# A second attention with stationary values, normalised before the turn, and four small changes

## The reference, cut to what matters

```
q, k, v = x @ wq[e].T, x @ wk[e].T, x @ wv[e].T
attn    = softmax(where(mask, q @ k.T / 4, -1e30))
outs[e] = (attn @ v) @ wo[e].T
fused   = concatenate(outs)
result  = silu(fused @ w_gate.T) * (fused @ w_up.T)
```

## Time and profile before

| | us |
|---|---|
| median of 3 runs | 416.32 |
| lowest, highest | 416.05, 422.2 |
| the profiled execution | 418.84 |
| its span, first to last instruction | 417.0 |
| TensorE busy | 398.4 (96%) |
| VectorE busy | 239.5 (57%) |
| ScalarE busy | 171.4 (41%) |
| GpSimd busy | 50.8 (12%) |

### The profile page before, as it was taken

The page is one execution under the profiler, slowest core; times in us unless marked ns, Lnnn a source line. Parts: engine busy times, 40 slices in busy tenths (PEclk is TensorE's granted clock), DMA queues, the critical chain, the costliest instruction groups (busy, mean ns, idle before and its releaser), DMA issues.

```text
span 417.0 us, 7793 instructions
## 1 busy us (share of the span) xinstructions
PE 398.4 (96%) x3100; PEld 332.8 (80%) x3100; DVE 239.5 (57%) x734; ACT 171.4 (41%) x290; POOL 50.8 (12%) x107
## 2 busy tenths in 40 slices
PE   8999999998899999999999989999999999999993
PEld 8978888787568767686747778998998999869783
DVE  1567656613368676777456387576558304687353
ACT  1246441742466546453513663354233320551420
POOL 7134010340000000100001310000000200304002
PEclk9999999999999999999999999999999989999998
DMA  7999600000299000000000997044221000000001
GB/s 200 260 194 223 142 11 1 2 0 4 61 242 283 12 2 0 2 0 2 2 0 11 272 265 221 17 128 132 67 67 57 2 0 2 3 2 2 2 0 38
DMA packets 28658, 30.53 MB, mean 73 GB/s; under 512 B 4868, under 2 KB 24074, under 8 KB 28623
## 3 DMA queue, kind: packets, MB, share of 16 engines
q1 hardware_dynamic: 28072, 29.82, 29.1%
q10 hardware_dynamic: 390, 0.22, 0.2%
q0 software_dynamic: 160, 0.01, 0.0%
HBM read 29.63 MB, written 0.39 MB: 72 GB/s over the span
## 4 chain that ended last, share of the span: by engine, by line
PE 83%; DVE 7%; ACT 3%; DMA 2%; issue 2%; POOL 1%; SPq 0%; DVEq 0%; POOLq 0%
PE ps L1474 75%; PE ps L1478 7%; DMA front<-in_x 2%; PE ps L1486 2%; DVE bn L984 1%; DVE wide L1349 1%; POOL rstd L509 1%; DVE mv L987 1%; ACT front L670 1%; DVE xn L999 1%; DVE front L1136 0%; DVE front L1135 0%; ACT front L686 0%; ACT front L766 0%; DVE front L1129 0%
## 5 line engine op out<-in xcount | busy, mean ns | idle before, releaser
L1474 PE MATMUL ps<-halves 128*128 128x512 f32 (+1 forms) x360 | 80.5, 378 | 1.3 <-ACT front L716 1.3
L1474 PE MATMUL ps<-front 64*64 64x64 f32 (+3 forms) x912 | 71.7, 265 | 5.1 <-ACT front L772 1.4
L1474 PEld LDWEIGHTS ps<-front 64*64 64x64 f32 (+2 forms) x912 | 64.9, 166 | 13.8 <-issue 4.4
L1474 PE MATMUL ps<-wide,front 128*128 128x192 f32 x432 | 73.7, 332 | 0.0
L1474 PEld LDWEIGHTS ps<-halves 128*128 128x128 f32 x360 | 63.0, 188 | 13.1 <-ACT front L716 1.7
L1474 PEld LDWEIGHTS ps<-wide,front 128*128 128x128 f32 x432 | 72.0, 194 | 1.0 <-issue 0.5
L716 ACT ACTIVATE front<-ps,colc 128x512 f32<-128x512 f32 x60 | 39.6, 688 | 53.0 <-PE ps L1474 52.9
L1478 PE MATMUL ps<-ident,front 128*128 128x128 f32 (+1 forms) x192 | 28.6, 276 | 0.7 <-DVE front L1149 0.4
L1296 DVE SCALAR_TENSOR_TENSOR xn<-ps,small,xn 128x192 f32<-128x192 f32 x28 | 9.8, 410 | 29.7 <-PE ps L1474 29.7
L1478 PEld LDWEIGHTS ps<-ident,front 128*128 128x128 f32 (+1 forms) x192 | 21.2, 138 | 6.3 <-issue 3.0
L1474 PE MATMUL ps<-xT,turned 128*64 128x256 f32 (+1 forms) x96 | 24.0, 474 | 1.5 <-ACT turned L656 1.5
(11 more groups left out here) (268 smaller groups left out, 537.9 us busy)
## 6 DMA issues: line engine op xcount, KB each, us to landing
wide<-in_w SPq DMA_DIRECT2D x8, 576.0 KB, 4.6
wide<-in_w SPq DMA_DIRECT2D x8, 384.0 KB, 6.0
wide<-in_w SPq DMA_DIRECT2D x16, 192.0 KB, 6.3
front<-in_a2w SPq DMA_DIRECT2D x5, 576.0 KB
front<-in_a1w SPq DMA_DIRECT2D x5, 384.0 KB
front<-in_x SPq DMA_DIRECT2D x3, 512.0 KB, 7.8
front<-in_w_qkv SPq DMA_DIRECT2D x2, 576.0 KB, 7.5
front<-in_a1w SPq DMA_DIRECT2D x5, 192.0 KB
```

Of the source, the lines that this page charges most:

```text
L1474: return pe.matmul(o, l, r, start=start, stop=stop)
```

## The change

Second attention. The values are stationary now, in 64x32 tiles (64 keys of one image, a pair's 32 features of which 16 are zeroed for the other head), and the turned probabilities of one head and one image move, 64 columns. So the output is written already turned. It has no column of sums: VectorE normalises the exponentials before they are turned. Scores run two steps ahead, `p1` has three buffers, `oT1` has two, and the first projections of expert 1 stand before the loop.

```diff
-        vbd = take(2, NT, PAIRS, 2, 2 * DH + 1)
+        vz = take(2, NT, PAIRS, 2, 2 * DH)
-        p1 = take(2, PAIRS, 2, S)
+        p1 = take(3, PAIRS, 2, S)
-        oT1 = take(2, T)
+        oT1 = take(2, 2, T)
...
 @@ scalar
+            def oT_out(n):
+
+                e, t = divmod(n, NT)
+                act.wait_ge(s["pv1_mm"], n + 1)
+                if e >= 2 and t == 0:
+                    act.wait_ge(s["wo1_mm"], 2 * (e - 1))
+                act.activation(oT1[0:96, e % 2, :, t * P:(t + 1) * P].rearrange("p c (m i) -> p c m i", m=2),
+                               ps[0:96, 6:8, 0:P].rearrange("p m (c i) -> p c m i", c=2),
+                               ACT.Copy).then_inc(s["oT1_done"], 1)
...
+            qk_out(1, 1)
+            qk_out(1, 0)
+            exp1(1)
             N1 = NT * EA
             for n in range(N1):
                 pT1_out(n)
                 if e < EA - 1:
-                    if t == 0:
-                        qk_out(e + 1, 1 if e == 0 else 0)
-                    elif t == 2:
+                    if t == 0 and e >= 1:
+                        qk_out(e + 1, 0)
+                    elif t == 1:
                         qk_out(e + 1, 2)
                     elif t == 3:
                         v_out(e + 1, 0)
-                if t == 1 and e >= 1:
-                    fT_out(e - 1)
-                if n + 1 < N1:
-                    exp1(n + 1)
+                if n + 2 < N1:
+                    exp1(n + 2)
...
+                if e >= 1 and t == (2 if e < EA - 1 else 0):
+                    fT_out(e - 1)
+                oT_out(n)
 @@ vector
+            def softmax1_out(n):
+
+                x = n % 2
+                pk = p1[:, n % 3].rearrange("p a m j -> p (a m) j")
+                dve.wait_ge(s["exp1"], n + 1)
+                link(dve.tensor_reduce(mx1[:, x, :], pk, AX.X, ALU.add))
+                link(dve.reciprocal(mx1[:, x, :], mx1[:, x, :]))
+                dve.tensor_tensor(pk, pk, mx1[:, x, :].unsqueeze(2).to_broadcast([P, 2 * PAIRS, S]),
+                                  ALU.mult).then_inc(s["p1_done"], 1)
...
             softmax1_in(0)
+            softmax1_in(1)
+            softmax1_out(0)
             N1 = EA * NT
-            for n in range(N1):
-                e, t = divmod(n, NT)
-                if n + 1 < N1:
-                    softmax1_in(n + 1)
-                if n % 2 == 0 and n >= 2:
-                    oT_out(n // 2 - 1)
-                if t == 1 and e >= 1:
-                    fT_low(e - 1)
-                out1(n)
-            oT_out(2 * EA - 1)
+            for n in range(N1 - 1):
+                if n + 2 < N1:
+                    softmax1_in(n + 2)
+                softmax1_out(n + 1)
 @@ tensor
-                if x == 0 and e == 0:
+                if x == 1 and e == 0:
                     pe.wait_ge(s["wt_act"], EA)
-                if x == 1 and e == 0:
                     pe.wait_ge(s["wt_dve"], EA)
...
             def turn1(n):
-                pe.wait_ge(s["exp1"], n + 1)
+                pe.wait_ge(s["p1_done"], n + 1)
...
             def values1(n):
                 e, t = divmod(n, NT)
                 pe.wait_ge(s["pT1_done"], n + 1)
-                pe.wait_ge(s["v1_done"], 2 * e + 1 + t // 2)
+                pe.wait_ge(s["v1_done"], 2 if n == 0 else 2 * e + 1 + t // 2)
                 if n >= 1:
-                    pe.wait_ge(s["o1_done"], n)
-                w = 2 * (2 * DH + 1)
-                for p in range(PAIRS):
-                    ins = mm(ps[:, 7, p * w:(p + 1) * w], pT1[:, n % 2, p, :],
-                             vbd[:, e % 2, t, p].rearrange("p m d -> p (m d)"), True, True)
+                    pe.wait_ge(s["oT1_done"], n)
+                for c in range(2):
+                    for h in range(2):
+                        for g in range(3):
+                            p = 3 * c + g
+                            for m in range(2):
+                                r = slice(DB * m, DB * m + DB)
+                                ins = mm(ps[32 * g:32 * g + 32, 6 + m, S * c:S * (c + 1)],
+                                         vz[r, e % 2, t, p, h, :], pT1[r, n % 2, p, S * h:S * (h + 1)], h == 0, h == 1)
                 ins.then_inc(s["pv1_mm"], 1)
...
             values_in(0, 1)
+            scores1(1)
+            project1(1, 1)
+            project1(1, 0)
             for n in range(N1):
-                if n + 1 < N1:
-                    scores1(n + 1)
-                if n == 0:
-                    project1(1, 1)
+                if n + 2 < N1:
+                    scores1(n + 2)
                 turn1(n)
                 if e < EA - 1:
-                    if t == 0:
+                    if t == 0 and e >= 1:
                         project1(e + 1, 0)
-                        if e >= 1:
-                            project1(e + 1, 1)
-                    elif t == 2:
+                        project1(e + 1, 1)
+                    elif t == 1:
                         project1(e + 1, 2)
+                    elif t == 2 and e >= 1:
+                        join(e - 1, 0)
+                        join(e - 1, 1)
                     elif t == 3:
                         values_in(e + 1, 0)
                         values_in(e + 1, 1)
-                if n >= 1:
-                    turn_o(n - 1)
-                if t == 1 and e >= 1:
+                elif t == 0:
                     join(e - 1, 0)
                     join(e - 1, 1)
-                if e == EA - 1 and t >= 2:
-                    gate_up(t, first)
+                elif t < 3:
+                    gate_up(t + 1, first)
+                else:
+                    pe.wait_ge(s["s1_read"], N1)
+                    gate_up(0, first)
                 values1(n)
-            pe.wait_ge(s["s1_read"], N1)
-            gate_up(0, first)
-            turn_o(N1 - 1)
             gate_up(1, first)
             join(EA - 1, 0)
             join(EA - 1, 1)
```

```diff
+            def values_wide(i):
+
+                pe.wait_ge(s["wv_lo"], 1)
+                pe.wait_ge(s["v0_done"], 3 + i)
+                at, o = slice(i * P, (i + 1) * P), ps[:, 2, 0:3 * P]
+                mm(o, xs0.high[:, at], wvx.high, True, False)
+                mm(o, xs0.high[:, at], wvx.low, False, False)
+                mm(o, xs0.both[:, at], wvx.both, False, False)
+                mm(o, xs0.low[:, at], wvx.high, False, False)
+                mm(o, xs0.lowB[:, at], wvx.both, False, True).then_inc(s["v0_mm"], 1)
...
             for hp in range(PAIRS - 1):
+                if hp in (2, 3):
+                    values_wide(2 * hp - 4)
                 project0(hp + 1)
-                values_in0(hp + 1)
+                if hp + 1 < 3:
+                    values_in0(hp + 1)
+                elif hp in (2, 3):
+                    values_wide(2 * hp - 3)
```

```diff
+            for i in range(NT):
+                for k in range(2):
+                    ins = mm(two_t(6, i), xT[:, k, i * P:(i + 1) * P], wos[:, k, :], k == 0, k == 1)
...
-            keep_busy(25, 2)
+            keep_busy(10, 2)
...
-                    ins = dve.scalar_tensor_tensor(tok[:, i, :], tok[:, i, :], rstd[:, i:i + 1], xn[:, i, :],
+                    ins = dve.scalar_tensor_tensor(tok[:, i, :], two_t(6, i), rstd[:, i:i + 1], xn[:, i, :],
...
+            for c in range(2):
+                link(dve.bn_stats(bn[:, c, :], wvo3[:, 1, c, :]))
+                link(dve.bn_aggr(mv[:, c, :], bn[:, c, :]))
+                ins = dve.scalar_tensor_tensor(wos[:, c, :], wvo3[:, 1, c, :], mv[:, c, 0:1], bc["ln_w"][:, :],
+                                               ALU.subtract, ALU.mult)
```

```diff
-            finish(0)
+            added(0, 2)
+            moments(of(tok), 0)
+            centre(of(tok), of(xn), 0, done="fin_ready")
             dve.wait_ge(s["cls_mm"], 1)
...
-            finish(1)
+            added(2, 1)
+            moments_one(2)
+            added(3, 1)
+            moments_one(3)
+            centre_one(2)
+            centre_one(3)
```

More of the change, by code:

```diff
@@ L137, in vit_tower @@
         mx0 = take(2, B)
+        v0w = take(NT, 3 * P)
         take = carve(front[:, 9600:])
@@ L589, in _ @@
             rsqrt(0, 96, 1)
-            rsqrt(1)
+            rsqrt(1, n=1)
+            rsqrt(1, n=1, first=3)
         @block.scalar
@@ L900, in _ @@
             send(act, 6)
-            send(act, 7)
         @block.vector
@@ L2145, in _ @@
             pe.wait_ge(s["m0_in"], 64)
-            down(hT[:, 0], m0w2, 4, halves=True, tiles=range(2))
+            down(hT[:, 0], m0w2, 4, tiles=range(2), each=True)
             pe.wait_ge(s["selm_done"], 1)
@@ L2155, in _ @@
             ins.then_inc(s["cls_mm"], 1)
-            down(hT[:, 0], m0w2, 4, halves=True, tiles=range(2, NT))
+            down(hT[:, 0], m0w2, 4, tiles=range(2, NT), each=True)
 _INS = {
```

254 lines of the change are left out of this document (122 added, 132 removed).

## The result

The changed kernel takes 412.5 us (median of four runs, 409.79 to 413.96), the kernel before beside it 416.75: a ratio of 0.9865, 95% interval 0.983 to 0.990, so about 1.3% faster, which is less than the 2% that the prediction took for the least that can be told from no change; the interval does exclude no change. Two later groups of runs gave 0.983 (0.979 to 0.987) and 0.9866 (0.983 to 0.991). The profiled execution took 411.31 (span 409.6) against 418.84 (417.0); predicted was 413.2 for it and 411 for the median. One part of the luck is in the executions that were profiled: the pair differs by 7.5 us, the medians of the same group by 4.25, and the ratio stands for 5.6.

What follows compares the result with a forecast made beforehand. TensorE, busy 96% of the span, was taken to bound the kernel. Gains of 3.6 + 1.3 + 0.6 + 0.1 = 5.6 us took the profiled 418.84 to 413.2, the median to 411; range 407.5 to 416, held at 0.8.

Steps and rivals of the forecast that it cites:

- Start of the second attention: Second attention: first projection no longer waits for weight copies, scores at 108.75 instead of 112.02; first turn 117.75, head start spent.
- part 2's 1.3: First attention: wide fp32r value products replace narrow ones, gain 1.3 us, so everything later starts that much sooner.
- The later signs: Second attention: first turns of experts 1 and 3 expected at about 138.0 and 185.1.
- The values: Second attention, each step: 48 records in 64x32 tiles at 22.7 ns, 1.10 us; bounds 1.04 and 1.90.
- rival B: Second attention: small tiles cost 39.5 ns per record, 8 us more in ten steps, 419 in all; chance 0.05.
- VectorE's step: Second attention: VectorE takes 5.26 us per step, 5.4 with two handoffs, from the end of scores to the next turn.
- Step by step: Second attention: expert 0 takes 21.55 us, experts 1 and 2 together end at 186.4, last join at 213.6; gain 3.6.
- a clock of 0.50 inside expert 0: Second attention, expert 0: listed among the signs that would make the forecast wrong, without a size.
- rival A: Second attention: clock falls at 102.8 (1.5), handoffs cost more (1.4), tiles cost 1.29 (1.9); 4.8 back, 415.6; chance 0.25.
- First attention: Wide value records at 160 ns: steps 2 and 3 gain 0.35 each, step 4 1.2; ScalarE delay 0.64; net 1.3.
- Norm of the retention: Layer norm of the last attention: joining 1.05 us earlier, less about 0.45 for making the centred weight; gain 0.6 us.
- Finish: End of the kernel, finishing per tile: last DMA issue at 415.3 against 415.4, gain 0.1 us.

Runs made afterwards that it cites:

- the kernel before with the wait moved: Kernel before, with only the first projection of the second attention no longer waiting for the last weight copies: 415.28 us, 0.9916 of the kernel before.
- undisturbed profile: Profile of the changed kernel run again unaltered, in which the clock did not fall in expert 0: 411.09 us, 0.983 of the kernel before.
- wait: Changed kernel whose first projection of the second attention waits again for the last weight copies: 413.89 us, 0.9907 of the kernel before.
- values: Changed kernel with the first attention's values of pairs 3 to 5 made pair by pair in fp32 as before: 412.8 us, 0.9887 of the kernel before.
- norm: Changed kernel with the retention's scaled products back on VectorE, 25 filler products and no centred weight: 411.42 us, 0.9844 of the kernel before.
- row order: Changed kernel with each step's 48 small records reordered so that neighbours share their half of the rows: 409.38 us, 0.981 of the kernel before.
- early projection: Changed kernel with expert 1's third projection and its ScalarE copies one step sooner, no filler: 411.54 us, 0.979 of the kernel before.
- half multiplication: Changed kernel with VectorE normalising only 32 of every 64 probabilities, part of the computation left out: 406.82 us, 0.971 of the kernel before.
- the two kernels with filler: Changed kernel with unused products in expert 0's waits (409.91 us, 0.9775), and with every hole filled plus the third projection sooner (409.22 us, 0.978).
- the four variants of the second group: Changed kernel with weight wait restored (0.9907), narrow first-attention values (0.9887), retention's norm back on VectorE (0.9844), or small records reordered (0.981).
- The kernel with filler but one larger hole left: Changed kernel with filler ahead of turns and expert 1's third projection one step sooner, no filler ahead of the third turn: 411.63 us, 0.982.

## Why the prediction was right, and where it was right by luck

**Start of the second attention: right.** The first scores end at 107.62 (108.75 less part 2's 1.3 was said), the first turn starts at 116.64 (116.4). VectorE's two inputs and one output ahead of the first turn spend the head start: 16.66 us from the first projection to the first turn in each of the three profiles of the changed kernel, 13.12 in the kernel before with the wait moved. The later signs were met less well: the first turns of experts 1 and 3 were due at 138.0 and 185.1 and came at 139.17 and 183.99 in the first profile, one late by the clock, one early by the cheaper steps.

**The values: the term of the sum that was mis-sized.** 1.10 us per step were taken, 0.74 was measured, below the lower bound of 1.04, which came from 64x64 tiles; rival B (39.5 ns) is out. By the distance of starts it is less still, 0.67 (198.65 to 199.32 in the first profile). The Trainium skill, TensorEngine Tiling (Array Packing), Key Properties, says that switching the mode drains the engine, and I had put an estimate of 0.1 us per step beside it. The trace agrees: where a piece in full 128x128 tiles stands ahead of the new products, its distance to the next piece grew by 0.10, from 3.43 to 3.53 for the two projections (138.61 to 142.14) and from 2.60 to 2.70 for the values' projection. Behind the third projection (1.87 for 1.88) and the join (3.67 both times) nothing was added; these ran in 128x64 and 96x128 tiles. That draining is what the 0.10 is made of no run shows.

**VectorE's step: 5.4 taken, 5.10 measured.** Its timeline in the undisturbed profile never waits:

```profile
116.93 0.75 DVE L1164 TENSOR_TENSOR front<-ps,causal 128x256 f32<-128x256 f32 x2
117.60 0.41 DVE L1166 TENSOR_TENSOR front<-ps,causal 128x256 f32<-128x256 f32 x1
118.05 0.95 DVE L1170 TENSOR_REDUCE front<-front 128x12 f32<-128x768 f32 x1
119.03 0.96 DVE L1171 TENSOR_TENSOR front<-front 128x768 f32<-128x768 f32 x1
119.91 0.95 DVE L1179 TENSOR_REDUCE front<-front 128x12 f32<-128x768 f32 x1
120.89 0.23 DVE L1180 RECIPROCAL front<-front 128x12 f32<-128x12 f32 x1
121.15 0.96 DVE L1181 TENSOR_TENSOR front<-front 128x768 f32<-128x768 f32 x1
122.03 0.75 DVE L1164 TENSOR_TENSOR front<-ps,causal 128x256 f32<-128x256 f32 x2
```

122.03 - 116.93 = 5.10. The subtraction and the multiplication have 0.96 as their length, but what follows starts 0.88 after them; and the two handoffs (0.14) are hidden by the second step of depth. Lengths overlap: a sum over a queue that never waits has to be made from starts.

**Step by step, undisturbed.** From first turn to first turn expert 0 took 20.83 for 21.55 predicted; experts 1 and 2 22.40 each for 23.55 (steps of 5.78, 5.35, 5.92, 5.35 for 6.2, 5.4, 6.55, 5.4: the values in two of them, and joining, with 3.67 + 1.54 instead of 3.70 + 2.04); expert 3 to its join about 22.1 for 23.5. The second step of an expert, 5.35 for VectorE's 5.4, matches by luck: what ends TensorE's wait of 1.00 us there is ScalarE's copy of the third projection (L745), and ScalarE's copies stood in the prediction with 0. Where that projection comes a step sooner the step takes 5.09. Together the second attention gains 7.8 against a kernel before that has its wait and its slow stretch at 101 to 106, 4.2 more than the 3.6 predicted. That is counted from the end of the weights' turns (101.38 before, 100.41 in the undisturbed profile) to the last join:

```profile
213.51 3.74 PE L1474 MATMUL ps<-front,turned 96*128 96x512 f32 x8
```

```profile
204.78 3.74 PE L1510 MATMUL ps<-front,turned 96*128 96x512 f32 x8
```

**What gave it back: a clock of 0.50 inside expert 0.** The prediction named it as a thing that would make it wrong, and gave it no price there (rival A had put it at 102.8). It takes 1.70, 1.70, 2.0, 2.2, 3.1 and 3.9 us in the six profiles that show it with the third projection in the changed kernel's place. Of the nine profiles with holes left open in expert 0 throughout (the changed kernel three times, wait, values, norm, row order, early projection, half multiplication) seven show it, two don't; both profiles with all larger holes from the first turn on filled or shortened to 0.9 us or less don't (one had the hold of 1.40 us there and kept the clock); the one with a single larger hole left open shows it just there. Profiles are few, but every run has its mean granted clock on record: 0.987 or more in all twelve runs of the two kernels with filler, and in 11 of the 43 runs of the changed kernel and of the four variants of the second group, whose holes are open. The kernel with filler but one larger hole left has it in none of six. (The mean takes in the falls elsewhere too, and the share differs: 3 of 16 in the changed kernel, 4 of 6 with the row groups apart, and 5 of 6 with half of the multiplication, whose waits are open but up to 0.4 us shorter.) So filling TensorE's waits of 0.7 to 2.0 us, one after another in four steps, keeps the fall away; why the same holes bring it in one execution and not in the next stays open.

**First attention: right for the wrong reason.** The hold gave 0.5 of the 1.33. The mis-sized term: a wide record was priced at 160 ns, from ten of 512 columns in 2.14 us. But those 2.14 are a length: the next piece began 2.41 after the first load, 241 ns each. In the changed kernel the first timeline has

```profile
38.48 1.95 PE L1510 MATMUL ps<-front,xT 128*128 128x128 f32 x16
40.27 0.60 PE L1514 MATMUL ps<-ident,front 128*128 128x128 f32 x4
...
42.40 4.34 PE L1510 MATMUL ps<-halves 128*128 128x384 f32 x20
46.58 0.60 PE L1514 MATMUL ps<-ident,front 128*128 128x128 f32 x4
```

4.18 us for ten of 512 and ten of 384 columns, so 1.8 for the latter, as much as the sixteen narrow ones (40.27 - 38.48): steps 2 and 3 gain 0.1 together, not 0.35 each. Step 4 gains 1.0 (1.2 said), and the value products wait 0.23 for ScalarE, not 0.64.

**Norm of the retention: 0.6 said, 0.08 measured.** Joining started 0.76 sooner, not 1.05, since VectorE's moments and its join now wait for TensorE's products (0.39 and 0.49 us):

```profile
371.07 0.63 DVE L1015 BATCH_NORM_STATS2 bn<-ps 128x6 f32<-128x192 f32 x2 [0.39 <-PE ps L1510]
...
372.47 0.74 DVE L1399 SCALAR_TENSOR_TENSOR tok<-ps,rstd,xn 128x192 f32<-128x192 f32 x2 [0.49 <-PE ps L1510]
```

The 0.45 for the weight was right (0.44), but the small wait that it makes ahead of the turns of the last expert's rows costs 0.24 more in the turns themselves. **Finish: 0.1 said, 0.4 to 0.5 measured.** The last centring ends 7.6 us after the last product piece began, as said. The last issue of a transfer ends 8.9 after it (SP's now, 9.2 before and ScalarE's); the other 0.2 lies in what follows the issues and wasn't traced further.

**What stays open.** In all twelve profiles of the changed kernel and its variants the clock falls to 0.50 around the retention's values (3.24 to 3.91 us instead of 2.72, so 0.5 to 1.2), in the two based on the kernel before it isn't. Putting back the norm, the first attention's values or the wait doesn't change that. GpSimd's copies and the finish weren't tried.

## What to carry to other kernels

When an edit moves work from TensorE to an engine that then sets the step, price the holes that open on TensorE too: each costs nothing by itself, but here they brought the lower clock to the work between them in most executions, and filler products in them took the bad runs away. A duration that matches in one pair of profiles proves little while a hold of up to 1 us comes in one execution and not in the next: compare intervals between landmarks in several profiles. Price a tile shape that no trace has with wide bounds, and queues that never wait by the distance of starts.

## What the runs showed of the hardware that was not expected

A record of a 64x32 tile with 64 columns moving costs 15.4 ns when neighbours alternate between the halves of the rows, 19.0 in the order of the run with row groups apart; 64x64 tiles cost 21.6 and 128x32 tiles 22.7. Ahead of the 64x32 products a piece in full tiles takes 0.10 us more. TensorE stands still for 0.3 to 1.4 us with no wait that the profile shows, mostly once near 48 us, in twelve of the fourteen profiles, and elsewhere at most once. The gate stages have a slow stretch of the clock too (near 330 to 340 us), in nine of fourteen profiles, kernel before included: 141.86 us from last join to the turn of the last expert's rows with it, 140.18 without, 1.7 us for one fall. In all nine it falls at the end of or just behind sixteen short records with 8 and 3 rows (from 327.31 in the first profile, where the clock is 0.54 in 330 to 332); the other five profiles have the same records and keep the full clock. Falls in expert 0 (1.7 to 3.9 us), in the gate stages (1.7) and the hold at 48 us (up to 1) are together enough for the 4 us by which runs of one kernel differ; which run had which is known only for those profiled.
